# Query exponentials taken head by head on ScalarE, and four small statistics moved to other engines

## The reference

```python
# end of layer 2: out is a mixture of two experts' rows, then normed and added to x
mu = out.mean(-1, keepdims=True); var = out.var(-1, keepdims=True)
out = (out - mu) / jnp.sqrt(var + EPS) * ln_g + ln_b

# attention of layer 3 (8 heads of 64), on x normed over its features
q = layer_norm(x @ Wq, ln_q_g, ln_q_b)
k, v = split(context @ Wkv)          # and one null key and value per head
q = softmax(q, axis=-1) * 8          # over the 64 features of a head
k = softmax(k, axis=2)               # over the keys
out = (q @ (k^T v)) ; out = layer_norm(out, ln_out_g, ln_out_b) @ Wout
x = x + tanh(gate) * out
```

## Time and profile before

| | |
|---|---|
| median of three runs | 1692.73 us |
| profiled execution | 1684.34 us, its span 1682.4 us |
| share of the span, busy | PE 73%, VectorE 58%, GpSimd 51%, ScalarE 43% |
| the stretch of this pipeline with keys in it | 1036 to 1343 us from the span's start |

### The profile page before, as it was taken

The page is one execution under the profiler, slowest core; times in us unless marked ns, Lnnn a source line. Parts: engine busy times, 40 slices in busy tenths (PEclk is TensorE's granted clock), DMA queues, the critical chain, the costliest instruction groups (busy, mean ns, idle before and its releaser), DMA issues. The chain is left out here.

```text
span 1682.4 us, 36100 instructions
## 1 busy us (share of the span) xinstructions
PE 1230.4 (73%) x11766; PEld 989.2 (59%) x11766; DVE 968.6 (58%) x2844; ACT 720.6 (43%) x1710; POOL 850.2 (51%) x1105
## 2 busy tenths in 40 slices
PE   3888874918888697654199984787788844999991
PEld 2666653916766474444088873565666633888881
DVE  3887861247999576477322225667778931444444
ACT  2765641416888253452044434444444421222222
POOL 1447564516776134456344445557777762333334
PEclk9998986967999798775599997899999966999996
DMA  5322203624332002011477753000000002222215
GB/s 133 104 93 88 74 14 103 200 74 128 105 111 65 13 2 65 4 40 46 130 198 212 201 150 90 2 1 12 14 15 15 18 28 78 57 81 63 75 37 154
DMA packets 156236, 130.04 MB, mean 77 GB/s; under 512 B 21530, under 2 KB 133932, under 8 KB 156080
## 3 DMA queue, kind: packets, MB, share of 16 engines
q1 hardware_dynamic: 144816, 106.98, 22.4%
q0 software_dynamic: 11264, 21.07, 3.7%
HBM read 89.77 MB, written 40.57 MB: 77 GB/s over the span
## 5 line engine op out<-in xcount | busy, mean ns | idle before, releaser
L1342 POOL DMA_INDIRECT l_rows_out<-l3e_y,l3e_target x80 | 77.6, 970 | 176.9 <-DVE l3e_y L1330 164.7
L1298 ACT ACTIVATE l3e_sT<-l3e_ps_h 128x256 f32<-128x256 f32 x160 | 61.5, 384 | 178.2 <-PE l3e_ps_h L1269 149.9
L1342 POOL DMA_INDIRECT l_rows_out<-l2e_y,l2e_target x80 | 77.8, 972 | 103.7 <-DVE l2e_y L1328 91.5
L1316 DVE TENSOR_TENSOR l3e_hT<-l3e_sT,l3e_ps_h 128x256 f32<-128x256 f32 x160 | 67.4, 421 | 99.1 <-ACT l3e_sT L1298 99.1
L1295 ACT ACTIVATE l2e_hT<-l2e_ps_h,l2e_b 128x256 f32<-128x256 f32 x160 | 69.9, 474 | 107.7 <-PE l2e_ps_h L1264 107.7
L1268 PE MATMUL l3e_ps_h<-l3e_xT,l3e_w 128*128 128x256 f32 x320 | 100.9, 397 | 4.9 <-DVE l3e_xT L1307 0.6
L1269 PE MATMUL l3e_ps_h<-l3e_xT,l3e_w 128*128 128x256 f32 x320 | 96.4, 383 | 0.0
L1066 POOL DMA_INDIRECT l_rows_in<-l2a_rt_rows,l2f_slot x64 | 62.8, 981 | 57.3 <-DVE l2f_slot L1056 40.0
L1278 PE MATMUL l2e_ps_y<-l2e_w,l2e_hT 128*128 128x128 f32 x640 | 78.9, 277 | 0.0
L1278 PE MATMUL l3e_ps_y<-l3e_w,l3e_hT 128*128 128x128 f32 x640 | 78.0, 275 | 0.0
L1264 PE MATMUL l2e_ps_h<-l2e_xT,l2e_w 128*128 128x256 f32 x320 | 77.5, 386 | 0.6 <-DVE l2e_xT L1307 0.6
(11 more groups left out here) (521 smaller groups left out, 3758.0 us busy)
## 6 DMA issues: line engine op xcount, KB each, us to landing
l2e_w<-in_L_ffn_w SPq DMA_DIRECT2D x80, 256.0 KB
l1a_side<-in_fside_Bx16xSxS SPq DMA_DIRECT2D x32, 512.0 KB, 3.6
l0e_w<-in_L_ffn_w SPq DMA_DIRECT2D x32, 256.0 KB
l_rows_in<-l0a_fill_rows SPq DMA_DIRECT2D x14, 528.0 KB, 2.7
l_rows_out<-l0a_fill_rows SPq DMA_DIRECT2D x12, 512.0 KB, 3.5
l3e_w<-in_L_ffn_W SPq DMA_DIRECT2D x24, 256.0 KB
l2e_rows<-l_rows_in SPq DMA_DIRECT2D x40, 132.0 KB, 3.2
l3e_rows<-l_rows_in SPq DMA_DIRECT2D x40, 132.0 KB, 2.2
```

The source lines that it names most:

```text
L1298: nc.scalar.activation(sT[:, f % 2, :], ps_h[f % 2][:, 0:CHUNK], act_func).then_inc(s_ready, 1)
L1316: nc.vector.tensor_tensor(hT[:, b, f, :], sT[:, f % 2, :], ps_h[2 + f % 2][:, 0:CHUNK], ALU.mult).then_inc(h_ready, 1)
L1342: pool.indirect_dma_start(out=r.rows_out, out_offset=bass.IndirectOffsetOnAxis(ap=target[:, c % 2, a:a + 1], axis=0), in_=y[:, c % 2, a, : ...
```

## The change

- GpSimd's `query_centred` (32 instructions of 128 x 512) goes. ScalarE takes each head's exponential from `qb` directly, with the head's column of `nmq` as bias: 8 instructions of 128 x 64 in place of one of 128 x 512. `nmq` has two buffers. VectorE's `query_offset(t)`, which rewrites a buffer of `qb`, now waits for the exponentials of tile t - 2 instead of for GpSimd.
- `x_eps_of` moves from the end of VectorE's turn (tile i + 5) to ScalarE's, after the copy of turned keys (tile i + 4). It becomes an activation with a pointer bias.
- `output_variance` moves from VectorE to ScalarE, after `values`.
- `offset` moves from VectorE to GpSimd, behind `rstd`, with one more small instruction (`gap`, the negated mean).
- `query_variance` becomes a tensor_scalar whose second scalar is `eps` as a pointer.

```diff
-            pool.tensor_tensor(qc[:, :, :], qb[:, t % 2, :, :], nmq[:, :].unsqueeze(2).broadcast_to([P, H, HD]), ALU.add
-                               ).then_inc(s["qc_ready"], 1)
...
-            pe.wait_ge(s["pq_ready"], t + 1)
+            pe.wait_ge(s["pq_ready"], H * (t + 1))
...
-            act.wait_ge(s["qc_ready"], t + 1)
+            act.wait_ge(s["mq_ready"], t + 1)
             reused(act, s["qT_ps"], t)
-            nc.scalar.activation(pq[:, :], qc[:, :, :].rearrange("p h d -> p (h d)"), ACT.Exp).then_inc(s["pq_ready"], 1)
+            for h in range(H):
+                nc.scalar.activation(pq[:, h * HD:(h + 1) * HD], qb[:, t % 2, h, :], ACT.Exp, bias=nmq[:, t % 2, h:h + 1]).then_inc(s["pq_ready"], 1)
...
+        pool.tensor_scalar(self.gap[:, q % 2, :], self.moments[:, at, 0], -1.0, None, ALU.mult).then_inc(s["veps_ready"], 1)
+        pool.wait_ge(s["veps_ready"], 2 * q + 2)
         pool.tensor_tensor(self.rstd[:, at], self.veps[:, q % 2, :], self.half[:, :], ALU.pow).then_inc(s["root_ready"], 1)
+        pool.wait_ge(s["root_ready"], q + 1)
+        pool.tensor_tensor(self.nmr[:, at], self.gap[:, q % 2, :], self.rstd[:, at], ALU.mult).then_inc(s["nmr_ready"], 1)
...
-        dve.wait_ge(self.s["x_mom_ready"], t + 1)
-        self.nc.vector.tensor_scalar(self.eps[:, t:t + 1], self.x_moments[:, t, 1:2], LN_EPS, LN_EPS * LN_EPS, ALU.mult, ALU.add
+        act.wait_ge(self.s["x_mom_ready"], t + 1)
+        self.nc.scalar.activation(self.eps[:, t:t + 1], self.x_moments[:, t, 1:2], ACT.Identity, scale=LN_EPS, bias=self.eps_squared[:, :]
...
-            V.scalar_tensor_tensor(out=var[:, t, 0:1], in0=qsq[:, t:t + 1], scalar=0.0, in1=before.eps[:, t:t + 1], op0=ALU.max, op1=ALU.add
+            V.tensor_scalar(var[:, t, 0:1], qsq[:, t:t + 1], 0.0, before.eps[:, t:t + 1], ALU.max, ALU.add).then_inc(s["ve_ready"], 1)
...
-            reused(dve, s["qc_ready"], t - 1)
+            reused(dve, s["pq_ready"], H * (t - 1))
...
-            V.tensor_reduce(nmq[:, :], qb[:, t % 2, :, :], AX.X, ALU.max, negate=True).then_inc(s["mq_ready"], 1)
+            V.tensor_reduce(nmq[:, t % 2, :], qb[:, t % 2, :, :], AX.X, ALU.max, negate=True).then_inc(s["mq_ready"], 1)
...
-            V.tensor_scalar(var[:, t + AHEAD, 1:2], mo[:, t, 1:2], LN_EPS, None, ALU.add).then_inc(s["vo_ready"], 1)
+            nc.scalar.activation(var[:, t + AHEAD, 1:2], mo[:, t, 1:2], ACT.Identity, bias=before.eps_once[:, :]).then_inc(s["vo_ready"], 1)
```

More of the change, by code:

```diff
@@ L1428, in __init__ @@
         self.veps, self.half = ph.sb("veps", [P, 2, 4]), ph.sb("half", [P, 4])
+        self.gap, self.eps_squared, self.eps_once = ph.sb("gap", [P, 2, 4]), ph.sb("eps_squared", [P, 1]), ph.sb("eps_once", [P, 1])
         self.rstd, self.nmr = ph.sb("rstd", [P, NT]), ph.sb("nmr", [P, NT])
@@ L1458, in prepare @@
         pool.memset(self.half[:, :], -0.5).then_inc(self.s["filled"], 1)
+        pool.memset(self.eps_squared[:, :], LN_EPS * LN_EPS).then_inc(self.s["filled"], 1)
+        pool.memset(self.eps_once[:, :], LN_EPS).then_inc(self.s["filled"], 1)
     def shift(self, dve):
@@ L1502, in root @@
         pool.wait_ge(s["mom_ready"], 4 * q + 4)
-        pool.wait_ge(s["filled"], 1)
+        pool.wait_ge(s["filled"], 3)
         pool.tensor_scalar(self.veps[:, q % 2, :], self.moments[:, at, 1], LN_EPS, None, ALU.add).then_inc(s["veps_ready"], 1)
-        pool.wait_ge(s["veps_ready"], q + 1)
+        pool.tensor_scalar(self.gap[:, q % 2, :], self.moments[:, at, 0], -1.0, None, ALU.mult).then_inc(s["veps_ready"], 1)
+        pool.wait_ge(s["veps_ready"], 2 * q + 2)
         pool.tensor_tensor(self.rstd[:, at], self.veps[:, q % 2, :], self.half[:, :], ALU.pow).then_inc(s["root_ready"], 1)
[L1508 to L1514, removed]
+        pool.wait_ge(s["root_ready"], q + 1)
+        pool.tensor_tensor(self.nmr[:, at], self.gap[:, q % 2, :], self.rstd[:, at], ALU.mult).then_inc(s["nmr_ready"], 1)
     def normal(self, act, t):
@@ L1545, in x_mean_of, with x_eps_of @@
         self.nc.vector.bn_aggr(self.x_moments[:, t, :], self.xbn[:, t % 4, :]).then_inc(self.s["x_mom_ready"], 1)
[L1547 removed]
+    def x_eps_of(self, act, t):
         if not self.is_tile(t):
             return
[L1551 to L1553 removed]
+        act.wait_ge(self.s["filled"], 3)
+        act.wait_ge(self.s["x_mom_ready"], t + 1)
+        self.nc.scalar.activation(self.eps[:, t:t + 1], self.x_moments[:, t, 1:2], ACT.Identity, scale=LN_EPS, bias=self.eps_squared[:, :]
+                                  ).then_inc(self.s["eps_ready"], 1)
 def ternary_ffn(nc, core, name, gate, wfcT_dram, wprojT_dram, ln_w, ln_b):
@@ L2060, in linear_programs @@
     qb = ph.sb("qb", [P, 2, H, HD])
-    nmq = ph.sb("nmq", [P, H])
-    qc = ph.sb("qc", [P, H, HD])
+    nmq = ph.sb("nmq", [P, 2, H])
     pq = ph.sb("pq", [P, I])
@@ L2429, in key_exponents, with output_variance @@
             nc.scalar.activation(ek[:, I:I + H], nmk[:, :], ACT.Exp, bias=nk[:, :]).then_inc(s["ek_ready"], 1)
+        def output_variance(t):
+            if not is_tile(t):
+                return
+            act.wait_ge(s["mo_ready"], t + 1)
+            nc.scalar.activation(var[:, t + AHEAD, 1:2], mo[:, t, 1:2], ACT.Identity, bias=before.eps_once[:, :]).then_inc(s["vo_ready"], 1)
+        act.wait_ge(before.s["filled"], 3)
         for k in range(EARLY):
@@ L2437, in scalar @@
             turned_keys(k - 1)
+            before.x_eps_of(act, i + 4)
             query_exponents(i + 1)
@@ L2443, in scalar @@
             values(k)
+            output_variance(i)
             before.scale(act, i + 17)
@@ L2567, in output_mean @@
             V.bn_aggr(mo[:, t, :], bo[:, :]).then_inc(s["mo_ready"], 1)
-        def output_variance(t):
-            if not is_tile(t):
-                return
-            dve.wait_ge(s["mo_ready"], t + 1)
-            V.tensor_scalar(var[:, t + AHEAD, 1:2], mo[:, t, 1:2], LN_EPS, None, ALU.add).then_inc(s["vo_ready"], 1)
         def residual(t):
@@ L2597, in vector @@
             query_maximum(i + 2)
-            before.offset(dve, quad(i + 12))
             query_squares(i + 4)
@@ L2607, in vector @@
             query_offset(i + 3)
-            output_variance(i)
             combined(k - 1)
@@ L2618, in vector @@
             summed(i - 1)
-            before.x_eps_of(dve, i + 5)
             router.choose(dve, quad(i - 4))
```

11 lines of the change are left out of this document (2 added, 9 removed).

## The result

The changed kernel takes 1713.24 us (median of 6 runs, 1708.23 to 1721.64) against 1694.19 before (6 runs, 1684.13 to 1698.48): ratio 1.0122, 95% interval 1.0088 to 1.0157, so 19 us more. 1714 was forecast. The profiled execution's span is 1714.3 us; before it was 1682.4, but 6.2 us of that difference lie ahead of the turns shown next, and that profiled execution was a quick one. The ratio is the measure, and the traces say where the time lies.

What follows compares the result with a forecast made beforehand. The prediction took a closed TensorE-ScalarE chain as the bound. Terms +42.7, +8.6, -14.3, -9.5 and -7 gave +20.5 us, plus 1.5 for the last exponentials: +22 on the 1692.73 median, so 1714, range 1700 to 1731.

Steps and rivals of the forecast that it cites:

- The chain: TensorE and ScalarE form a closed loop setting ordinary turns; added ScalarE work lengthens each one for one, by 1.78 us.
- The pieces: Eight ScalarE exponentials for one, between `kS` and `oT`: 1.92 us in place of 0.54, taken as +1.4 a turn.
- The two small ones: `eps` between `kS` and `oT`, output variance between the values' copy and `xnT`, on ScalarE: +0.19 us each per turn.
- The long turns: Once in four turns `oT` waits for `nmr`; the excess was to fall from 18 us to 3.7.
- the -14.3: Term for turns where `oT` waits for `nmr`: 3.7 us excess left instead of 18.
- The added `eps` wait: VectorE's query variance waits for ScalarE's same-turn `eps`, covered by 0.7 us; rival that it takes over: 1724 us, 12%.
- The running count: TensorE's wait for the router's count on GpSimd goes when the centring is removed: -9.5 us.
- The first two and the last six turns: Edges of the 31 turns: last six from 7.95 to 9.4 us each, +8.6; the opening turns got only the ordinary growth.
- the +8.6: Term for the last six turns, without `normal`, growing from 7.95 to 9.4 us each.
- The rival of 1744 us: More half clock: longer TensorE stands in ordinary turns slow ten more turns, +30 us; chance 10%.
- The sum: All terms over the 31 turns give +20.5 us, with +1.5 for the last two tiles' exponentials: +22.
- the two rules of the Trainium skill: Two-SBUF-input VectorE instructions wait for GpSimd (new form gains 0.45 us a turn or keeps the wait); additions belong on VectorE.

Runs made afterwards that it cites:

- e8: The kernel before with only the query variance changed to a tensor_scalar; ratio 0.9978 to the kernel before.
- e2: The kernel before with the eight per-head exponentials and no GpSimd centring, nothing else of the change; ratio 0.9990 to the kernel before.
- e3: The changed kernel with both `eps` and the output variance back on VectorE; ratio 0.9974 to the kernel before.
- e9: The changed kernel with only the output variance back on VectorE, `eps` staying on ScalarE; ratio 1.0073 to the kernel before.
- e1: The changed kernel with GpSimd's centring and the single whole-tile exponential put back; ratio 1.0123 to the kernel before.
- e4: The changed kernel with one 128 x 512 exponential straight from `qb`, leaving out the head's maximum; ratio 0.9988 to the kernel before.
- e5: The kernel before with ScalarE's `normal` and two scalings moved behind the copy of turned x; ratio 1.0002 to the kernel before.
- eA: The kernel before with `normal` and scalings behind turned x's copy, offset on GpSimd, query variance as tensor_scalar; ratio 0.9905 to the kernel before.
- e7: The changed kernel with the output variance ahead of the values' copy and `eps` at the turn's end, both on ScalarE; ratio 1.0005 to the kernel before.

## Why the prediction was right, and where it was not

*The chain.* Right. The ordinary turn grew by 1.75 (1.78 forecast), L2285 waits for `oT` in 30 turns (by 1.74 in ordinary ones, where 0.5 to 1.5 was forecast), and the shorter VectorE work shows in no turn (e8).

*The pieces.* Right in size: 0.34 us each, 1.91 from the first to `normal` where 1.92 were taken, e2 and e3 +1.38 a turn. The proportion between the 8-column and the 128-column row held at 64 columns.

*The two small ones.* Right in the ordinary turn, 0.19 and 0.20. The failed step is "Left on VectorE the two small ones would cost nothing, and the sum would be 11 us less": it would be 25 less (e3). The term held only their own length. It missed that the variance's place delays GpSimd's roots to 1.98 behind L2253, and that `eps` alone costs 17 (e9), of which a good part, turns at half clock, is explained by no run. The prediction did see that delay, 1.85, and counted it as a gain on the 2.35 of the earlier trace rows; it didn't ask what the long turn would be if the variance were earlier. The answer is e2 and e3: 10.5 on average, nearly without stall.

*The long turns.* Half right. L2285 was forecast 9.6 behind L2253; it came at 9.79 in the turn at 1271.97 and 9.76 in that at 1133.35. But the price of the 0.7 to 1.3 us left was set at their length, 3.7 us in all, and the clock made it more in four of the five turns that had such a wait: 12.30 us on average over the seven, with 0.81 and 0.91 granted in the two shown. The fifth (at 1091.18, where TensorE stood 2.67) kept 1.00 and took 11.24. Before, the sum of the long turns was 84.9; it is 86.1. Against that, the pieces and small ones put into them (7 x 1.78 = 12.5) and the -14.3 had promised 83.

*The added `eps` wait.* The cover was argued along the wrong path. L2552's output is turned by L2275 in the turn after, so this wait doesn't reach `oT` in the same turn; it reaches TensorE through `kc` (e1 and e4). That "`kc` is still done some 1.2 us ahead of L2264" held while the exponentials were long. The number stood because ScalarE's chain was the longer of the two. The query variance took 0.21 us and not 0.14, which costs nothing while VectorE has that room.

*The running count.* Right, gone; the turns after the long ones fell by 2.3 in all, where 7 x 1.78 - 9.5 gave +3.

*The first two and the last six turns.* An undisturbed one of the last takes 9.35 (9.4 forecast), but "go at the pace of VectorE" is wrong: 7.95 is the pace of TensorE with its stand for `xnT`, as e5 and eA show. The estimate of 7.95 was right by accident. And the +8.6 did not come: the six together grew by 1.2 us (56.0 to 57.2), since before they held 4.7 of waits for the running count, and one turn had only 0.86 of the clock. The first two turns grew by 4.5 us, with 0.69 and 0.81 granted where both had 1.00; the forecast had no term for them beyond the ordinary one.

*The clock.* The rival of 1744 us didn't come: the granted clock of the 31 turns is 0.94 after and 0.93 before. But this hides the point. Spaced a little differently, the same work ran at 0.97 to 0.98 (e2, e3), with TensorE 232.7 us busy in e3 against 242.1. That is one execution each; over all runs the clock of the whole span was 0.871 to 0.879 in e3 and 0.866 to 0.876 in the changed kernel, so the direction holds and the size is less sure. Of the 25.4 us between e3 and the changed kernel 9.4 are TensorE working slower, and 16 are TensorE standing.

*The sum.* +22 forecast, +19 measured, +24.7 in the 31 turns of the trace against +20.5. It was right on the whole change, and wrong on what its parts would do alone: without the two small ones it gave +11, and the runs gave nothing (e2) or -4.5 (e3). The removal of the centring was priced at the running count's 9.5 us; together with what it does in the long turns it is worth 15 to 23 (e1 to e4), and the pieces cost 20 to 23 where their ordinary turns gave 33 (24 x 1.38). The errors offset each other: that the total came within 3 us is in part luck.

Of the two rules of the Trainium skill, the second (ScalarE: Activation LUTs, "Rules for kernel authors": additions on VectorE, some 0.3 us for each activation) names the dearer engine, and the trace agrees with its figure (0.29 and 0.30 here), but not that this alone decides: e7 keeps both on ScalarE and costs nothing beside before. For the first (SBUF — State Buffer, "Who interferes with whom") e1's rows show the tensor_scalar of eight columns at 0.71 us beside GpSimd's L2155, against 0.22 at 1269.74 us in the changed kernel. The trace agrees that it can wait for GpSimd. For the query variance, sorted by whether a tensor instruction of GpSimd was running as it started, the form with two SBUF inputs took 142 ns in 14 cases without one and 888 in 18 with one (the kernel before); the one-column tensor_scalar took 198 in 13 and 191 in 19 (e8). So the trace agrees with the rule on two inputs, and the new form did not keep the wait.

## What to carry to other kernels

What a small instruction on an in-order queue costs here is not its own length but its place: behind something that waits for this turn's matmul, it passes that wait on to all who need its result, here to GpSimd and to a stall that came back only once in four turns. Price such a move twice, for the turns in which its consumer has time and for those in which it has none, and for each part of a change ask what the others hide: a total that comes out right does not show that its terms are. A chain that grows everywhere may cost nothing where the time between long stalls is used by the engine that was late (e2), so count by kinds of turn and not by the mean.
